# A graph network on one core: GpSimd issues gather k only when gather k-2 has landed in SBUF

## What is computed

```python
edge_index = jnp.stack([src, dst])
x = _layernorm(x + _L0_gnn_ref(x, edge_index, W_l, b_l, W_r))
#   L0: segment_sum((x @ W_l.T + b_l)[src], dst) / max(deg, 1) + x @ W_r.T
x = _layernorm(x + _L1_gnn_ref(x, edge_index, W_self, b_self, W_neigh, b_neigh, gamma, beta))
#   L1: neigh = segment_sum(h[dst] @ W_neigh.T + b_neigh, src) / max(deg, 1)
#       out = relu(h @ W_self.T + b_self + neigh); layernorm(h + out) * gamma + beta
```

## Time and profile before

| | |
|---|---|
| time, median of 3 runs | 3786.76 us (3784.0 to 3786.78) |
| the profiled execution, first to last instruction | 4265.6 us |
| gathers, both layers | 1856, each 128 rows of 2056 bytes |
| busy share of the span | TensorE 65%, VectorE 61%, GpSimd 44%, ScalarE 19% |
| first and last gather start, layer 0 | 518.2 and 1984.4 us |
| first and last gather start, layer 1 | 2391.1 and 3792.5 us |

### The profile page before, as it was taken

How to read it: one execution, slowest core, us unless ns; L and a number is a source line. 1 busy time by engine, 2 the same in 40 slices (tenths; PEclk the granted TensorE clock), 3 DMA queues, 4 the chain that set the end, 5 groups by cost and what they waited for, 6 DMA issues and landing times.

```text
span 4265.6 us, 57125 instructions
## 1 busy us (share of the span) xinstructions
PE 2781.9 (65%) x11308; PEld 1195.8 (28%) x11308; DVE 2610.8 (61%) x6523; ACT 815.1 (19%) x2156; POOL 1897.4 (44%) x2073
## 2 busy tenths in 40 slices
PE   1000188888888888866999655555555555568887
PEld 0000033333333333322455211112111111124443
DVE  3878877777777777754555444444444444448887
ACT  0300044444444444410222000000000000002222
POOL 0600166666666666664000366666666666630000
PEclk9555599999999999977999765665566665669999
DMA  3300066656656666664333566666666666671111
GB/s 140 121 0 0 25 166 166 167 162 165 166 164 164 166 167 166 165 203 136 98 103 103 156 175 178 173 175 173 175 176 176 175 174 170 168 115 59 59 59 49
DMA packets 201222, 586.38 MB, mean 137 GB/s; under 512 B 34672, under 2 KB 35502, under 8 KB 201196
## 3 DMA queue, kind: packets, MB, share of 16 engines
q0 software_dynamic: 148480, 488.56, 42.3%
q1 hardware_dynamic: 52716, 97.53, 7.3%
HBM read 534.51 MB, written 51.44 MB: 137 GB/s over the span
## 4 chain that ended last, share of the span: by engine, by line
PE 39%; DVE 19%; issue 16%; DMA 10%; DVEq 6%; another core or an unknown queue 4%; ACT 2%; SPq 2%; POOL 2%; POOLq 0%; ACTq 0%
PE ps L703 37%; DMA rows<-table,idx_ring 8%; DVE acc L577 4%; DVEq L571 3%; DVE flat L496 2%; DVE onehot L564 2%; POOL rows L359 2%; DVE flat L497 1%; DVE flat L498 1%; DVE where L592 1%; PE ps L805 1%; DVE st L651 1%; PE ps L808 1%; DVE spot L590 1%
## 5 line engine op out<-in xcount | busy, mean ns | idle before, releaser
L359 POOL DMA_INDIRECT rows<-table,idx_ring x1856 | 1794.6, 967 | 1438.0 <-issue 453.5
L703 PE MATMUL ps<-rows,onehot 128*128 128x512 f16 (+1 forms) x5568 | 1378.6, 384 | 782.5 <-DVE acc L577 614.7
L577 DVE TENSOR_TENSOR acc<-acc,ps 128x513 f32 x928 | 638.7, 688 | 850.8 <-remote 328.4
L703 PE MATMUL ps<-where,put 128*128 128x464 f16 x3328 | 801.1, 363 | 380.3 <-ACT put L852 297.8
L703 PEld LDWEIGHTS ps<-rows,onehot 128*128 128x128 bf16 x5568 | 537.3, 113 | 1645.9 <-DVE acc L577 749.2
L564 DVE TENSOR_SCALAR onehot<-iota_node,loc_ring,rows 128x128 bf16<-128x128 f16 x1856 | 583.4, 322 | 281.2 <-DMA rows<-table,idx_ring 250.1
L851 ACT ACTIVATE put<-spot,flat 128x128 f16<-128x128 f16 x832 | 334.1, 402 | 1099.4 <-DVE spot L590 754.3
L703 PEld LDWEIGHTS ps<-where,put 128*128 128x128 f16 x3328 | 267.4, 97 | 696.5 <-issue 371.3
L592 DVE TENSOR_SCALAR where<-iota_chunk,hi_ring 128x928 f16<-128x928 f16 x832 | 380.4, 457 | 0.0
L865 ACT ACTIVATE flat<-acc,rdeg 128x512 f32 (+1 forms) x98 | 69.4, 710 | 1577.5 <-DVE rdeg L640 1574.0
L703 PE MATMUL ps<-w_a,flat 128*128 128x512 f32 x784 | 355.1, 596 | 0.1
(11 more groups left out here) (131 smaller groups left out, 1368.0 us busy)
## 6 DMA issues: line engine op xcount, KB each, us to landing
rows<-table,idx_ring POOLq DMA_INDIRECT x1856
table<-rows SPq DMA_DIRECT2D x98, 257.0 KB, 3.7
h_scratch<-rows SPq DMA_DIRECT2D x49, 256.0 KB, 2.0
rows<-h_scratch SPq DMA_DIRECT2D x49, 256.0 KB, 2.7
acc<-in_x SPq DMA_DIRECT2D x4, 3072.0 KB, 23.5
rows<-in_x SPq DMA_DIRECT2D x48, 256.0 KB, 3.3
out<-rows SPq DMA_DIRECT2D x48, 256.0 KB, 2.0
w_a<-in_w_l_t SPq DMA_DIRECT2D x1, 1024.0 KB
```

The costliest lines, as they stand in the source:

```text
L359: nc.gpsimd.indirect_dma_start(out=rows[:, k % GB, :], out_offset=None, in_=tables[layer][:, :], in_offset=bass.IndirectOffsetOnAxis(ap=id ...
L577: V.tensor_tensor(tile_acc, tile_acc, part, ALU.add).then_inc(s_acc, 1)
L703: return nc.tensor.matmul(*args, skip_group_check=True, **kw)
```

## The change

Ahead of the waits that each gather had, GpSimd now waits until the gather two before it has landed: `s_row` of that gather's slot at the value which its landing brings. The first two gathers of layer 0 go without; in layer 1 the first two wait for the last two of layer 0. Nothing else in the kernel differs (lines below move by 8, so L359 becomes L367).

```diff
--- before.py
+++ after.py
@@ -348,6 +348,14 @@
                         if k % H == 0:
 
                             pool.wait_ge(s_idx, (layer * CHUNKS[0]) // H + 2 * i + k // H + 1)
+                        if not (first and k < 2):
+
+                            n = (k - 2) % U
+                            landed = 16 * (chunk0(layer) // GB + U // GB * (i if k >= 2 else i - 1) + n // GB + 1)
+                            if not isinstance(landed, int):
+                                landed = pool.to_reg(landed)
+                            pool.wait_ge(s_sel, 2)
+                            pool.wait_ge(s_row[n % GB], landed)
                         if not (first and k < GB):
 
 
```

## The result

The changed kernel takes 5413.24 us (median of 4 runs, 5409.98 to 5414.44) against 3786.77 before (3786.76 with one run fewer, as above): 1.4292 times as long, 95% interval 1.4272 to 1.4312. The prediction had the direction and the mechanism, with 5150 us and a range up to 5300; the time lies 263 us above the one and 113 above the other.

A forecast was written before the change was run, and what follows sets the result against it. Before: GpSimd's issue bounds layer 1, TensorE layer 0's sorting part, 2391 us of gathers. Landing, release, instructions and dispatch make 4.08 and 4.03 us per two gathers, 3763 us: 5159, given as 5150 us; range 4740 to 5300.

The forecast's parts named there:

- The bound before: Unprofiled gather stretches: GpSimd's issue at 1.25 us per gather in layer 1, TensorE at 1.335 us in layer 0's sorting part.
- The sum of 2391 us: Both layers' gather stretches before the change, unprofiled: 1280 us at GpSimd's pace plus 1111 us at TensorE's.
- the holes: GpSimd idling about 3 us after late VectorE additions in the recorded execution; absent unprofiled, hidden under landings after the change.
- The wait binds on every gather, two under way, nothing else in the loop: GpSimd's new wait: landing takes 3.49 us, two gathers later is 2.50 us, so every gather waits.
- The cycle, 4.08 and 4.03 us: Time for two gathers in layers 0 and 1: landing 3.01 or 2.96, release 0.25, GpSimd instructions 0.10, dispatch 0.72 us.
- The dispatch of 0.72: GpSimd, from last wait to the gather's start: 0.72 us, hidden in regular rows, paid by each gather with the new wait.
- The sum: Gather stretches of 1893 + 1870 = 3763 us against 2391 unprofiled: +1372 us, 5159 us in all.
- The range: Whole run: up to 5300 us, for 0.15 us more in the cycle (139 us), and down to 4740 us.
- the dense row's 3.49: Start to landing of a gather in a dense row, 3.49 us; not used, as starts two us apart overlap only in parts.
- rival B: Gather landings are faster when nothing is recorded: cycles of 3.58 and 3.62 us, 4740 us in all; chance 0.20.
- Rival C: TensorE's clock stays at half speed in layer 0's sorting part, 2.47 us per chunk, about 5510 us; chance 0.07.
- The Trainium skill's 2.0 us plus bytes: Gather landing estimated as 2.0 us plus bytes at 436 GB/s, 2.60 us: pace 1.84 us, about 4800 us.

The follow-up runs named there:

- second profile: The kernel before, unchanged, profiled once more: span 3789.5 us, gather stretches 2391.1 us; measured 3791.38 us.
- k-1: Changed kernel, but each gather waits for the landing of the gather just before it, one under way at a time: 9339.42 us.
- k-3: Changed kernel, but each gather waits for the landing of the gather three before it instead of two: 4216.42 us.
- half rows: Changed kernel, but layer 0's gathers fetch 1028 bytes per row instead of 2056, from a table of zeros: 5158.88 us.

## Why the prediction was right, and where it failed

- *The bound before.* Right in kind: GpSimd's issue in layer 1 (1.27 us for each gather, where it had 1.25), and in the sorting part TensorE, busy 961.98 of the 1000 us from 600 to 1600 in the second profile, at 1.31 us where it had 1.335. The sum of 2391 us was met because these two errors cancel. It also expected the changed kernel's recorded execution to have the holes, hidden under the landings; it has none.
- *The wait binds on every gather, two under way, nothing else in the loop.* Right, by the chain after, by the 910 and 894 starts of 926 that follow their landing at once, and by the runs with k-1 and k-3.
- *The cycle, 4.08 and 4.03 us.* This is the step that failed: the measured ones are 4.32 and 4.34. Over all gathers of the trace after, for layers 0 and 1: the last of a gather's 80 packets ends 3.07 and 3.08 us after the start in the mean, where I had 3.01 and 2.96 from one isolated row each. From there to the release it is 0.32 and 0.31 us, where I had 0.25: VectorE's start of 0.31 us after a landing was nearly all release, with little of its own in it. From release to the next start it is 0.93 and 0.96 us, where I had 0.10 + 0.72. The dispatch of 0.72 was right; ahead of it stand 0.18 us and not 0.10, as the steps between the register instructions count too; the last 0.03 and 0.05 are nearly all a pause of GpSimd that comes back every 106 gathers (last section). No single term was far out; all three were too small.
- *The sum.* 0.24 us in layer 0 and 0.31 in layer 1 over 464 cycles each would be 111 and 144 us: 255 of the 263 that were missing. The rest is that the prediction's own sum of 5159 us was given as 5150.
- *The range.* It took the cycle as known to 0.15 us, from one row for each layer. A cycle is paid 928 times, so 0.1 us in it is 93 us, and the room of 139 us was less than the 0.24 and 0.31 us that the cycle was off. Leaving out the dense row's 3.49 was right as to crowding (3.36 us with one under way and 3.40 with two, start to release); what the bound lacked was the spread among uncrowded gathers. The room was given to rival B instead.
- *Rival B, faster landings without the profiler.* Wrong: the median is 5413 us and not 4740, and in every kernel with the wait the profiled span is within 6 us of the median of its runs.
- *Rival C, the clock.* Didn't come: the clock was at 0.98 of full speed in the sorting part, at a busy share of 1193.76 / 1792 = 0.67. In layer 1 the clock stayed at half speed throughout (0.50, before 0.61); TensorE's 946.55 / 928 = 1.02 us for a chunk stayed under the 2.17 us from one gather to the next, so this cost nothing.
- *The Trainium skill's 2.0 us plus bytes* ("DMA: Bandwidth & Descriptors", the anatomy of one DMA on the SWDGE path) gave an estimate of 2.60 us for a landing. The chains here have 3.3 us from start to release. Its split into a fixed part near 2 us and one that grows with the bytes fits the half rows, read with that same straight line (2.1 and 1.2 us); its rate of 436 GB/s doesn't, as 263 KB in 1.2 us are 220 GB/s for these scattered rows.

## What to carry to other kernels

A wait that ties an issue to an earlier landing turns a stream into a loop: price it as the whole way around (start to landing, release, what the issuing engine still has to do, its dispatch), divided by the number of issues that the loop spans, and compare that with the pace of the stream. Four under way nearly hid a loop of some 4.6 us behind 1.25 us, three didn't. What an engine does ahead of time costs nothing in a stream and its full length in such a loop, and a pause that the stream didn't show can come out in the loop, so put the wait that is met last in time as the last one in the code.

A term that is paid a thousand times needs the mean of many rows, not one clean row, and a profile whose span doesn't match its runs needs a second one before anything is built on the difference.

## What the runs showed that was not expected

- GpSimd's dispatch of a gather takes 0.72 us from its last wait to its start, 0.51 of it before the sequencer goes on. In the kernel before this is invisible in rows 0.30 us apart.
- GpSimd pauses at regular distances. Its timeline in layer 1 of the changed kernel:

```profile
3232.43 0.94 POOL L367 DMA_INDIRECT rows<-table,idx_ring  x1 [4.22 <-issue]
3233.67 0.95 POOL L367 DMA_INDIRECT rows<-table,idx_ring  x1 [0.30 <-issue]
...
3461.09 0.94 POOL L367 DMA_INDIRECT rows<-table,idx_ring  x1 [4.12 <-issue]
3462.34 0.95 POOL L367 DMA_INDIRECT rows<-table,idx_ring  x1 [0.30 <-issue]
```

  These are 228.7 us and 106 gathers apart, and one start is 2.5 us later than the 1.6 us of idling usual there (0.6 and 1.6 alternate). The release of the gather came in time; from it to the start it is 3.48 us where it is 0.90 otherwise. There are 17 of them in the changed kernel, about 40 us together. They go by the number of gathers and not by time: in the kernel with k-1 two of them are at 5483.42 and 5935.96 us, 452.5 us and again 106 gathers apart, and the count runs on from layer 0 into layer 1. In the undisturbed profile of the kernel before, the starts at these places of layer 1 are 1.25 us apart like the others. What GpSimd does in them isn't known.
- Limiting gathers to one at a time hardly shortens a landing: the cycle is 4.28 us alone and 4.33 with two, start to release 3.36 and 3.40.
- A wait for the landing of k-4, met most of the time, still cost 1.4%, more than half of it by those pauses.
